# One of four quadrant moves handed from SyncE's queue to ScalarE's, and row block 0 split where it is used, in a fused attention and FFN kernel

## What is computed

```python
xn = _layernorm(x)
scores = jnp.einsum('bskgd,btkd->bkgst', qh, kh) * scale
scores = jnp.where(causal, scores, jnp.finfo(scores.dtype).min)
probs = jax.nn.softmax(scores, axis=-1)
attn = jnp.einsum('bkgst,btkd->bskgd', probs, vh)
s = attn.reshape(...) @ w_dense.T
g = _silu(_L0_ffn_ref(xn, k0, s0, k1, s1, k2, s2))
return x + s * g
```

## Time and profile before

| | us |
|---|---|
| median of 3 runs | 943.5 |
| lowest and highest | 942.27, 948.25 |
| the profiled execution | 943.73 |
| its span in the trace | 941.5 |

### The profile page before, as it was taken

The page is one execution under the profiler, slowest core; times in us unless marked ns, Lnnn a source line. Parts: engine busy times, 40 slices in busy tenths (PEclk is TensorE's granted clock), DMA queues, the critical chain, the costliest instruction groups (busy, mean ns, idle before and its releaser), DMA issues.

```text
span 941.5 us, 15708 instructions
## 1 busy us (share of the span) xinstructions
PE 905.5 (96%) x4272; PEld 761.8 (81%) x4272; DVE 664.4 (71%) x1163; ACT 509.4 (54%) x1077; POOL 464.4 (49%) x372
## 2 busy tenths in 40 slices
PE   7697999999999999999999999999999999999997
PEld 6586887888888788878888888888888788888885
DVE  7464866777666785777667885777677786688853
ACT  3454644646555754655456654656456564555641
POOL 5144534554445553555355463455355453345764
PEclk9998999999999999999999999999999999999999
DMA  6468463876549555675548645686547745455462
GB/s 211 114 181 212 101 144 83 223 187 136 122 109 268 136 122 124 184 207 133 134 112 253 154 114 125 155 236 139 140 104 231 175 112 125 132 153 129 99 171 112
DMA packets 204805, 143.58 MB, mean 152 GB/s; under 512 B 23152, under 2 KB 172144, under 8 KB 204784
## 3 DMA queue, kind: packets, MB, share of 16 engines
q1 hardware_dynamic: 204784, 143.32, 59.1%
HBM read 63.70 MB, written 23.20 MB: 92 GB/s over the span
## 4 chain that ended last, share of the span: by engine, by line
issue 46%; PE 25%; POOL 25%; SPq 1%; DVE 1%; DMA 1%; ACT 1%; POOLq 0%; DVEq 0%
POOL pt_lo L753 17%; POOL w_lo L763 4%; PE ps_m L1094 3%; PE ps_m L1095 3%; PE ps_m L1096 3%; POOL wd_lo L763 3%; PE ps_m L1226 2%; PE ps_o L1094 2%; PE ps_s L1094 2%; PE ps_o L1096 2%; PE ps_o L1095 2%; PE ps_s L1095 2%; PE ps_s L1096 2%; SPq L683 1%; PE ps_s L1211 1%
## 5 line engine op out<-in xcount | busy, mean ns | idle before, releaser
L753 POOL TENSOR_TENSOR pt_lo<-pt_lo,pt_hi 128x512 fp32r<-128x512 f32 x248 | 328.1, 1347 | 397.3 <-ACT pt_hi L841 396.9
L934 DVE CUSTOM_DVE_ANT_0 ps_s<-ps_s,mask 128x32 f32<-128x32 f32 (+31 forms) x256 | 181.5, 714 | 118.9 <-PE ps_s L1096 115.5
L841 ACT ACTIVATE pt_hi<-pt_lo 128x512 fp32r<-128x512 f32 x288 | 169.8, 626 | 116.9 <-DMA pt_lo<-turned 65.5
L1094 PE MATMUL ps_m<-xn_hi,w_hi 128*128 128x512 f32 (+1 forms) x388 | 152.8, 394 | 0.4 <-DVE q_lo L1042 0.4
L1095 PE MATMUL ps_m<-xn_lo,w_hi 128*128 128x512 f32 (+1 forms) x388 | 151.3, 390 | 0.0
L1096 PE MATMUL ps_m<-xn_hi,w_lo 128*128 128x512 f32 (+1 forms) x388 | 151.1, 389 | 0.0
L1094 PE MATMUL ps_s<-k_hi,q_hi 128*128 128x480 f32 (+15 forms) x384 | 128.3, 334 | 9.4 <-ACT prob_odd L805 8.3
L1094 PE MATMUL ps_o<-pt_hi,v_hi 128*128 128x512 f32 x288 | 115.4, 401 | 15.2 <-POOL pt_lo L753 15.2
L1095 PE MATMUL ps_s<-k_lo,q_hi 128*128 128x480 f32 (+15 forms) x384 | 128.6, 335 | 0.0
L1096 PE MATMUL ps_s<-k_hi,q_lo 128*128 128x480 f32 (+15 forms) x384 | 128.2, 334 | 0.0
L805 ACT ACTIVATE prob_odd<-ps_s,small 128x160 f32<-128x160 f32 (+15 forms) x128 | 95.2, 747 | 51.8 <-DVE small L934 50.5
(11 more groups left out here) (99 smaller groups left out, 1414.1 us busy)
## 6 DMA issues: line engine op xcount, KB each, us to landing
inv_rows<-inv SPq DMA_DIRECT2D x64, 256.0 KB, 3.5
pt_lo<-prob_odd SPq DMA_DIRECT2D x128, 128.0 KB, 2.4
pt_lo<-prob_even SPq DMA_DIRECT2D x128, 112.0 KB, 2.3
raw<-wqkv SPq DMA_DIRECT2D x48, 256.0 KB, 3.3
pt_lo<-prob_odd SPq DMA_DIRECT2D x128, 96.0 KB, 2.2
pt_lo<-prob_even SPq DMA_DIRECT2D x128, 80.0 KB, 2.2
raw<-wd SPq DMA_DIRECT2D x32, 256.0 KB, 5.1
turned<-prob_odd SPq DMA_DIRECT2D x32, 256.0 KB, 5.0
```

Of the source, the lines that this page charges most:

```text
L753: pool.tensor_tensor(pt_lo[:, slot, :], pt_lo[:, slot, :].bitcast(F32), pt_hi[:, hi_slot, :], ALU.subtract).then_inc(land_lo, 1)
L841: act.activation(pt_hi[:, hi_slot, :], pt_lo[:, LAND_AT[i % BLOCKS] + j, :].bitcast(F32), ACT.Copy).then_inc(land_hi, 1)
L934: dve.tensor_tensor_reduce(out=scores, in0=scores, in1=mask[:, S - width(i % BLOCKS, tile):S], scale=-1.0, scalar=BIG, op0=ALU.add, op1=AL ...
L1094: pe.matmul(out, sta_hi, mov_hi, start=start, stop=False)
```

## The change

First, `ACT_HEADS = (3,)`: of the four transfers of a part of row blocks 4 to 7, SP issues three and ACT's queue the fourth, by a new item `amove.i.b` in ACT's table. Second, row block 0's halves are made by `hi.land.0.0` and `lo.land.0.0` in the pass that weighs them, instead of by `land.8.0` at the end of the one before; the cases for row block 8 fall away. Third, all tables of `BODY` and `LAST` are written in another order.

```diff
+ACT_HEADS = (3,)
...
-    act += hi(*values) + hi(("land", first, 0))
+    act += hi(*values)
...
-    pool = lo(*split) + [("zero_odd",)] \
-        + lo(("land", first, 0))
+    pool = lo(*split) + [("zero_odd",)]
...
-        hi.weigh.7 hi.land.8.0
...
+        exp.5.1 hi.land.3.1 hi.land.3.2 hi.land.3.3 amove.4.0 exp.5.2 amove.4.1 amove.4.2
...
-                        for h in range(HEADS):
+                        for h in range(HEADS - len(ACT_HEADS)):
                             sp.dma_start(pt_lo[b * Q:(b + 1) * Q, slots, h * P:(h + 1) * P].bitcast(F32),
                                          prob_quadrants(i)[h * Q:(h + 1) * Q, :, b, :])\
                               .then_inc(landed[i % 2], 16)
...
+                    if what == "amove":
+                        i, b = item
+                        act.wait_ge(flipped, r.flip_no(i, b))
+                        if b == 0:
+                            act.wait_ge(block_weighed, WEIGHED0 + PAIRS * g + LAND_AFTER[i])
+                        slots = slice(LAND_AT[i], LAND_AT[i] + i + 1)
+                        for h in ACT_HEADS:
+                            act.dma_start(pt_lo[b * Q:(b + 1) * Q, slots, h * P:(h + 1) * P].bitcast(F32),
+                                          prob_quadrants(i)[h * Q:(h + 1) * Q, :, b, :])\
+                               .then_inc(landed[i % 2], 16)
+                        continue
...
-                        hi_slot = 0 if i == BLOCKS else pair_no(i, j) % HI_RING
-                        if j == COLUMNS[i % BLOCKS][0]:
+                        hi_slot = pair_no(i, j) % HI_RING
+                        if j == COLUMNS[i][0]:
```

More of the change, by code:

```diff
@@ L187 @@
+        scores.8.1 weigh.7.5 vblocks.0 weigh.7.6 weigh.7.7 dense.6.0 dense.6.1 scores.8.2
+        dense.6.2 dense.6.3 scores.8.3 dense.7.0 dense.7.1 dense.7.2 dense.7.3
     """,
     "act": """
[L189 to L192, removed]
@@ new lines @@
+        hi.split.q1 hi.split.q2 hi.split.q3 hi.split.k hi.weigh.0 exp.4.0 hi.land.2.0 hi.land.2.1
+        exp.4.1 hi.land.2.2 exp.4.2 hi.weigh.1 hi.split.v exp.4.3 hi.vblocks.1 exp.5.0 hi.land.3.0
+        exp.5.1 hi.land.3.1 hi.land.3.2 hi.land.3.3 amove.4.0 exp.5.2 amove.4.1 amove.4.2
+        amove.4.3 exp.5.3 hi.weigh.2 exp.6.0 hi.land.4.0 hi.unit.q0.0 hi.land.4.1 hi.land.4.2
+        hi.land.4.3 amove.5.0 amove.5.1 amove.5.2 exp.6.1 exp.6.2 hi.land.4.4 amove.5.3 hi.weigh.3
+        exp.6.3 hi.land.5.0 hi.land.5.1 hi.land.5.2 hi.land.5.3 exp.7.0 hi.land.5.4 amove.6.0
@@ L216 @@
+        flip.6.1 max.7.1 flip.6.2 flip.6.3 mul.weigh.4 max.7.2 max.7.3 lo.dense.3 lo.weigh.4
+        flip.7.0 flip.7.1 flip.7.2 lo.land.6.4 lo.unit.k.0 mul.weigh.5 flip.7.3 lo.weigh.5
+        lo.land.6.1 lo.unit.q2.0 inverse.6 inverse.7 lo.unit.q3.0 lo.dense.4 lo.land.7.1
+        lo.unit.q1.0 mul.weigh.6 lo.land.7.4 lo.dense.5 lo.weigh.6 max.8.0 lo.land.7.7 max.8.1
+        lo.vblocks.0 mul.weigh.7 max.8.2 lo.weigh.7 lo.dense.6 max.8.3 flip.8 inverse.8 lo.dense.7
     """,
     "pool": """
-        lo.split.wd0 lo.split.wd1 lo.split.wd2 lo.split.wd3 lo.land.1.0 lo.land.1.1 lo.split.q0
@@ L230 @@
+        move.6.3 rr.5 move.7.0 move.7.1 move.7.2 move.7.3 rw.6 rw.7 rr.6 rr.7 dw.8 rw.8 dr.8 rr.8
     """,
@@ new lines @@
+        flip.6.1 max.7.1 lo.hidden.1.0.2 mul.weigh.4 flip.6.2 lo.weigh.4 flip.6.3 lo.hidden.1.0.3
+        max.7.2 inverse.6 max.7.3 lo.dense.3 flip.7.0 lo.hidden.0.1.0 flip.7.1 lo.hidden.0.1.1
+        flip.7.2 lo.land.6.4 lo.hidden.0.1.2 mul.weigh.5 flip.7.3 lo.hidden.0.1.3 lo.weigh.5
+        inverse.7 lo.land.6.1 lo.dense.4 lo.hidden.1.1.0 lo.hidden.1.1.1 lo.hidden.1.1.2
+        lo.land.7.1 lo.hidden.1.1.3 mul.weigh.6 gate.0 lo.weigh.6 gate.1 gate.2 lo.land.7.4 gate.3
+        lo.dense.5 gate.4 lo.land.7.7 gate.5 mul.weigh.7 lo.weigh.7 lo.dense.6 gate.6 lo.dense.7
@@ L306 @@
+        add_x.0 add_x.1 add_x.2 lo.land.7.5 add_x.3 lo.land.7.6 add_x.4 add_x.5 add_x.6
     """,
     "sp": """
[L308 to L311, removed]
+        load.k0 load.k1 load.k2 dw.1 rw.1 dr.1 dw.2 rw.2 rr.1 dr.2 dw.3 dr.3 rw.3 rr.2 move.4.0
```

222 lines of the change are left out of this document (106 added, 116 removed).

## The result

The changed kernel takes 961.0 us (median of 4 runs, 960.1 to 961.8) against 945.4 for the kernel before in the same session (942.3 to 948.3): a ratio of 1.0166, 95% interval 1.0127 to 1.0205. It is 1.7% slower; the forecast was 922.4.

What follows compares the result with a forecast made beforehand. PE, busy 96% of the span, was taken to bound the kernel, with most loss in two first-pass stops. From 943.7 us: first pass -19.8, other passes -8.5, last stretch -1, new waits +8, giving 922.4, range 917 to 930.

Steps and rivals of the forecast that it cites:

- The new waits: Waits the new order adds for PE, booked at 1.0 us a pass, bounds 0 and 2.5, +8 in all.
- What takes its place: Row block 6's first scores wait 0.5 us for ACT's exponentials; row block 1's row-sum fetch adds 0.5, each pass.
- part 1: Row block 0's copy leaves the loop's threshold, so PE's wait for row block 1's exponentials goes: -8.3 and -1.7 us.
- the best one: The profiled kernel's fastest pass, 105.8 us; the first pass, 125.6, was to come down to it: -19.8.
- the stop and its clock: First pass, at the loop's threshold: PE's 8.3 us wait for exponentials plus 1.7 us of slow clock after it.
- part 2: Reordering around row block 3 covers its weighing by 4 us; the 5.41 us stop and 3.1 of slow clock go.
- part 3: ACT issues a quarter of row blocks 4 to 7's moves; the last square lands 2.6 us earlier, nothing booked.
- mostly margin: Said of the moves' 2.6 us earlier landing: little of PE's 15.2 us of waits belongs to row blocks 4 to 7.
- I book nothing: The earlier landing of row blocks 4 to 7 from ACT's share of the moves enters the sum at no gain.
- Rival (b): Slower: ACT holds row block 6's scores back each pass, 2.5 us plus slow clock, 959 us; chance 0.10.
- rival (a): Only the threshold stop goes; new waits take what row block 3 gives: 933.7 us, up to 945; chance 0.27.
- four signs that would show it wrong: First pass above 112 us, passes 2 to 7 averaging above 107.5, loop clock below 0.98, ACT issues over 0.9 us.

Runs made afterwards that it cites:

- e1: Changed kernel, with the fetch of row block 1's inverse row sums moved ahead of row block 3's writes on SP's queue; 946.6 us, ratio 1.0089.
- e8: As e1, with row block 5's exponential 1 ahead of all four copies of row block 3 and exponential 2 ahead of the last two; 935.4 us.
- e6: Kernel before in its own order, with both the row block 0 and row block 3 edits and no moves by ACT; 925.7 us, ratio 0.9827.
- e13: Kernel before in its own order, with the edit at row block 3 alone; 930.7 us, ratio 0.9888.
- e5: The kernel before, unchanged, run and profiled again; 942.3 us, ratio 1.0008.
- e3: Kernel before with only row block 0's halves made in the pass that weighs them; 938.7 us, ratio 0.9997.
- e14: The same kernel as e3, run again for another profile; 935.1 us, ratio 0.9942.
- e2: Changed kernel in its new order, but SP issues all 16 moves and ACT none; 985.5 us, ratio 1.0498.
- e12: The repaired order of e8, but SP issues all 16 moves and ACT none; 966.9 us, ratio 1.0257.
- e10: As e1, with row block 5's exponentials 1 and 2 both ahead of all four copies of row block 3; 931.6 us, ratio 0.9895.
- e7: Kernel before, with the row-sum fetch moved behind row block 3's readback issue and writes; 976.8 us, ratio 1.0396.
- e11: Changed kernel, with one load of weights put between row block 3's writes and the row-sum fetch; 952.3 us, ratio 1.0148.
- e9: e6 plus ACT issuing the fourth transfer of each part of row blocks 4 to 7; 932.8 us, ratio 0.9912.

## Why the prediction was wrong

Two terms of the sum failed, in different measure. The new waits were booked at +8, 1.0 us a pass. With them passes 2 to 7 were to take 6 x 106.8 = 640.8 us, and they took 672.0: this is 31.2 of the 38 us between the forecast change of -21.3 and the measured +16.7 of the profiles. The first pass was to come down by 19.8, to 106.8 with its new wait, and took 114.6: 7.8 more.

**What takes its place: the term that decided, too small by far.** Both places were the right ones, at 1.0 us a pass together. The first, ACT's exponentials, was forecast at 0.5 us. In the changed kernel it is hidden behind the other; e1 shows it with 12.7 us in 12 waits, and removing nearly all of it was worth 11.1 us by the medians (e1 to e8), 1.4 a pass. The second is where the working failed. The prediction gave the fetch of row sums "about 1 us to spare" with no row and no sum for it. Behind four writes it starts some 3 us later and takes 7.3 us to land, where the median is 3.5, and the dense product waited 1.8 to 2.9 us a pass; undoing this was worth 7 to 14 us (after to e1). Margins were worked out for ACT and PE, and not for SP's queue, whose issues lengthen one another. The sum also took "for granted that the other places stay covered", and they did not: row blocks 6 and 7 wait for POOL in each pass, 10.5 us in passes 2 to 7.

**Row block 0 (part 1): right in the mechanism, too large.** The stop is gone and the readback was in time. The first exponential starts at 37.33 and is done by 37.7, where "by about 39.2" was forecast; 1.1 us of this is the shorter prologue. But the sum took the first pass all the way down to the best one. It came to 114.6 us, not under 109, and to 115.1 in e6 without the new waits of the changed order. What stands there in its place, in the changed kernel, is 6.0 us of named waits (2.6 at the dense product, 1.7 for POOL, 1.4 for a query, 0.3 for an exponential) and a stretch of slow clock; in e6 it is the two waits for a query, behind row block 1's writes and the `exp.3.0` that waits for them, which the stop had hidden. What the stop and its clock (-10.0) were worth depends on the pair that is compared: 5.3 us in the first pass from e13 to e6, 8 to 12 from e5 and before to e3 and e14.

**Row block 3 (part 2): right in the outcome, not in its times.** No wait for POOL at row block 3 in the changed kernel, and ACT waits only 1.57 us there in pass 4, against 6.23. But the readback did not go out at +11.4. Pass 4 of the changed kernel, SP, ACT and PE; row block 3's scores end at 392.01:

```profile
408.36 0.38 SPq L675 DMA_DIRECT2D pt_lo<-turned  x1
...
415.03 0.64 ACT L855 ACTIVATE pt_hi<-pt_lo 128x512 fp32r<-128x512 f32 x1 [1.57 <-DMA pt_lo<-turned]
...
421.40 0.40 PE L1108 MATMUL ps_o<-pt_hi,v_hi 128*128 128x512 f32 x1
```

It went out at +16.4, later than before (+13.7), behind the same long issues of SP's queue. It landed at +23.0 and not at +20.3, and row block 3 was weighed at +29.4 and not at +26.5. That it was covered all the same is partly luck: its flight was 6.7 us instead of 8.9, and PE came later too. Done alone in the order of before (e13) this part is worth 10.6 us. By the profiles passes 2 to 7 give 8.0 (645.1 us in e5, 637.1 in e13), where 8.5 was booked. The first pass gives 5.2 against before and 1.9 against e5, where 8.5 was booked: the stop there was 5.41 us in before and 2.90 in e5.

**The moves (part 3): the wrong word was "mostly margin".** 12 issues take 7.95 us at row block 4 in pass 6, as forecast (7.9), but 9.0 at row block 7. ACT's issue takes 0.59 to 0.60 us alone, inside the bounds, and the four of row block 7 in the last stretch take 3.88 together, with their waits for the flips. But "I book nothing" held for the order of before alone. The new order weighs row block 5 some 5 us earlier, as the prediction noted, and lives on the earlier landing: without it 24 to 31 us are lost (e2), and 29 to 32 in the repaired order (e12). No row of before could price that; e2 did. Where the order has that margin, ACT's issues cost 4 to 7 us and bring nothing.

The rule of the Trainium skill, "DMA: Bandwidth & Descriptors", section "Issuing engines are not separate DMA queues", says that a second issuer saves issue time only. The runs do not contradict that: with the split no transfer landed sooner after its issue, and those of row blocks 6 and 7 later (3.3 to 3.7 us against 2.3 to 2.4). The page also calls issue time usually small beside the transfer. For one transfer that is so here (0.66 us against 2.2 to 2.4 to landing, in the kernel before), but 16 in a row take 10.5 us. The prediction called the issue time "the longer of the two" by rows 8, which show issues alone.

**The sum and the rivals.** Forecast -21.3, measured +15.7 beside before's runs. Rival (b) had the sign, and its time (959) by luck: it put 3.7 us and more on row block 6's scores with a slow clock in every stretch, and the larger wait was the dense product of row block 1, 2.3 us in the mean, with a slow clock in four passes. The changed kernel repaired at both places is at 931.6. That this is near rival (a)'s 933.7 is luck too: both stops are gone in it, and the order's thin margins (15.4 us of waits for POOL in e10) take back part of what they gave. Of the four signs that would show it wrong, three came: a first pass above 112, passes 2 to 7 at 112.0 on average, and a clock of 0.97 in pass 3.

## What to carry to other kernels

Before a transfer that an in-order engine waits for is moved behind bulk writes on the same queue, add the issues that it now stands behind, and take its time from issue to landing from a row where it already stands behind such writes, not from its median. Then look in that engine's list at everything queued behind the wait. A reorder for one stop is best made as the smallest edit that moves that stop: two stops repaired in the old order gave 0.983, the same intent as a whole new order (with the moves) 1.017. An edit's worth depends on the order that it stands in: the split of the moves was worth 24 to 32 us in one and cost 4 to 7 in another, so it has to be tried in both.

## What was not expected of the hardware

- Behind row block 3's four writes to DRAM the next issue is often held: the issue of the row-sum fetch took 1.9 to 2.6 us in the changed kernel and 1.1 to 2.7 in e7, a load of weights 2.0 to 2.5 in e11. It is not always so: a load there took 0.6 to 2.2 us in the kernel before and 0.4 to 2.7 in e6, and behind row block 0's writes the next issue took 0.34. What decides it no run shows.
- ACT's issues run ahead of its engine and beside its copies, 0.59 to 0.60 us each and 0.70 apart. What stands behind them in the list waits for the last one, with the flip that this one waits for (e9).
- With a quarter of the transfers issued by ACT, SP's of row blocks 6 and 7 landed 3.3 to 3.7 us after their issue, in the profiles of all seven kernels with the split; without it 2.3 to 2.4. Which resource they share is not shown.
- A wait of 2 to 3 us at the same place was followed by TensorE's half clock in some passes and not in others: in the changed kernel after 2.57, 2.89, 2.55 and 1.95 us, and not after 2.09, 1.79 and 2.43. In passes 2 to 7 of e6, where PE has no wait above a us, the clock stayed at 1.00.
